# Two tables of step numbers moved, one step reordered and one VectorE job cut in three, in an attention and fp8 layer kernel

## The chip, the core and the metric

The kernel runs on one NeuronCore of a Trainium2 chip. The metric is the device time of one execution in microseconds (us), taken as the median of several runs. Engines are named as the profile names them: PE is TensorE (matrix products and transposes), DVE is VectorE, ACT is ScalarE, POOL is GpSimd, SP is SyncE, which here only issues DMAs. A program on one core has its own instruction order on each engine, and the engines meet through semaphores only.

## What is computed

The input is 8 sequences of 1024 tokens with 256 features. Two residual branches follow each other: attention with distances in hyperbolic space, and one fp8-quantised dense layer. Cut to what matters:

```python
def attn(x):                                   # x: (8, 1024, 256), already layer-normalised; 16 heads of 16
    q_h, k_h, v_h = (exp_map_at_origin(split_heads(x @ W.T), c) for W in (W_q, W_k, W_v))
    dist = poincare_distance(q_h, k_h, c)      # arccosh of 1 + 2c|q-k|^2 / ((1-c|q|^2)(1-c|k|^2))
    weights = softmax(-beta_pos * dist - attention_bias)
    out = log_map(exp_map(weights @ log_map(v_h)))
    return concat(out) @ W_o.T

def ffn(x):                                    # x: bfloat16, layer-normalised
    x_q = (x / s_in).astype(float8_e4m3fn)
    k_q = (kernel / s_k).astype(float8_e4m3fn)
    return ((x_q @ k_q) * (s_in * s_k)).astype(bfloat16) + bias

x = x + attn(layernorm(x))
x = x + ffn(layernorm(x))
```

## The kernel before

**Tiling.** The 8192 tokens are cut into 16 groups of 512 (`NG`, `GTOK`). For each group of query tokens there are 32 steps (`STEPS`): 4 groups of heads times 8 tiles of 128 keys (`KT`). So there are 512 steps, numbered n, and n is also written as group G and step s within the group.

**One step.** PE makes the distances of 128 keys to 512 queries for 4 heads: `distances(n, 0)` and `distances(n, 1)`, two products each (line L1100). ACT takes a logarithm of the 128x2048 tile (`log`, L1217) and then an exponential (`power`, L1224). PE then multiplies the weights with the values (`values`, L1115). ACT thus runs two long instructions for each step. Only where the data could bring an argument near zero are the products bounded first by DVE (`bound`, L1293, and `clamp`, L1302, "open" units of 4 steps); all other units are "closed", and DVE has no work of its own in the attention there. PSUM bank 6 collects the values. The distances use banks 0 to 5, and `distances(n + 1, 1)` and `distances(n + 2, 0)` may be written only when `log(n)` has read its banks (semaphore `freed`).

**The side work.** Beside this, PE has to turn and project the tokens of later groups and to finish earlier groups. All of it goes through the one PSUM bank 7, one use after another: PE fills it, DVE empties it (semaphores `b7_filled` and `b7_copied`), and a later fill waits until the copy before it has ended. The kinds of uses are: X (4 PE transposes of the normalised tokens, two uses a group), M (a projection of 128 tokens onto 384 columns, two products, eight uses a group), A and R (maxima, and transposes of query and key rows), S (the transpose of a finished group of heads' sums, always in steps 2, 10, 18 and 26), T, W, Q and Y (the finishing stage of an earlier group). In which slot each use stands is written by hand in tables: `PROJECT_USES` for groups 3 to 15, `SECOND_USES` for group 2, `FIRST_USES` for what is left of group 1, `FINISH_USES` for the last stage. Group n is projected while group n - 2 is in its steps, and for groups 3 on slot k is step k - 4, so that slot 4 is step 0. For group 2, worked on during group 0, slot and step have the same number. A use written as `(slot, BOTH)` is cut in two: half its products stand ahead of `values` and half behind. `(slot, 0)` puts it whole ahead of `values`, `(slot, 1)` whole behind. In a step without uses PE makes two products whose result nobody reads (`keep_busy`, L1138), except where the step is in `BARE`.

**DVE's order.** In its step n DVE does `rest(n - 1)`: first the copies out of bank 7 of step n - 1's uses, then the copy of the sums (`copy_sums`, L1308, every eighth step), then pieces of the finishing stage (`finish.vector`) and of the projection (`project.vector`), by their own slot numbers. The piece of the finishing stage in slot 33 (step 1) adds bias and residual (L782 and L785); slots 0 to 2 of the projection normalise the tokens (L570 to L581, `xn_rdy`), and X waits for slot 2. After step 12 of group 0 `setup.vector_kernel` quantises the dense layer's weights, seven DVE instructions one behind the other (L236, L109 to L112, L238, L239); its result is first needed when group 0 is finished, long after.

**Group 0.** At step 2 of group 0 PE does what is left of group 1: A 0, R 4 and A 1, all ahead of `values`, and `distances(4, 0)` comes behind R 4, since it reads the keys that R 4 turns. The two DVE pieces that normalise group 2's tokens (slots 0 and 1) come after the copies of that step, and slots 2 and 3 after step 3's.

## Time and profile before

| | us |
|---|---|
| median of 3 runs | 1964.94 |
| lowest and highest of them | 1962.69 and 1970.7 |
| the profiled execution, its own time | 1962.98 |
| its span in the trace | 1961.1 |
| ACT busy | 1865.9 (95%) |
| PE busy | 1750.4 (89%), granted clock 0.981 in the mean |
| DVE busy | 1144.5 (58%) |

The span is the time from the first to the last instruction, and 1.9 us lie around it. Busy time of PE is modelled, so its share says little of what PE could still take. An idle time in brackets stands in front of an instruction, and the arrow names what ended it. The granted clock is TensorE's: 1.00 is 2.4 GHz, 0.50 is 1.2 GHz, and a value between says that part of the stretch had the one and part the other.

### The profile page before, as it was taken

The page shows a single profiled execution, that of the slowest core. Times are in us where ns is not written, and L with a number is a line of the kernel's source. Part 1 is how long each engine was busy: PE and PEld are TensorE (multiplying, and loading weights), DVE is VectorE, ACT ScalarE, POOL GpSimd, SP SyncE. Part 2 cuts the span into 40 slices and gives each one's busy share as a digit, 9 for nine tenths or more (in the row PEclk, how much of TensorE's full clock was granted, in tenths as well). Part 3 has the DMA queues.
Part 4 walks back from the last instruction along what each step waited for, and adds up shares of the span by engine and source line. Part 5 has one row for each costly group of instructions (what it writes and reads, how often), then busy time and mean ns, then how long its engine had stood idle before and what let it go on. Part 6 is the DMA issues. An engine that isn't in the chain of part 4 may idle for free.

```text
span 1961.1 us, 29119 instructions
## 1 busy us (share of the span) xinstructions
PE 1750.4 (89%) x10579; PEld 578.4 (29%) x10579; DVE 1144.5 (58%) x2855; ACT 1865.9 (95%) x1094; POOL 12.9 (1%) x35
## 2 busy tenths in 40 slices
PE   7988989899898898989898898998989899899896
PEld 4323222222222222222222222222222222223234
DVE  7554565665656756565666656656565655513545
ACT  4889999999999799999998899999999999999993
POOL 2000000000000000000000000000000000000000
PEclk9899999999999899999999899999999999999998
DMA  1323222041302214022130321314022131401110
GB/s 57 114 75 115 61 87 93 23 135 44 127 31 87 71 44 136 23 101 79 43 115 22 103 76 44 114 44 136 23 103 77 44 103 44 125 27 39 44 55 23
DMA packets 112953, 142.52 MB, mean 73 GB/s; under 512 B 35692, under 2 KB 61549, under 8 KB 112749
## 3 DMA queue, kind: packets, MB, share of 16 engines
q1 hardware_dynamic: 112748, 140.13, 21.9%
q8 instruction: 88, 1.44, 0.3%
q14 instruction: 117, 0.95, 0.2%
HBM read 85.07 MB, written 55.05 MB: 71 GB/s over the span
## 4 chain that ended last, share of the span: by engine, by line
ACT 55%; PE 21%; issue 14%; DVE 6%; ACTq 2%; DMA 0%; DVEq 0%; SPq 0%
ACT U L1217 29%; ACT U L1224 26%; PE ps L1100 8%; PE ps L402 7%; PE ps L1115 5%; ACTq L1265 2%; DVE U L1302 1%; DVE U L1293 1%; PE ps L407 1%; ACT e L530 0%; DMA U<-in_L_attn_W_o_dram 0%; ACTq L1266 0%; DVE ss L536 0%; PE ps L171 0%; ACTq L1216 0%
## 5 line engine op out<-in xcount | busy, mean ns | idle before, releaser
L1224 ACT ACTIVATE U<-U 128x2048 f32<-128x2048 f32 x512 | 1017.4, 1990 | 0.3
L1217 ACT ACTIVATE U<-ps 128x2048 f32<-128x2048 f32 x500 | 975.7, 1951 | 20.1 <-PE ps L1100 17.6
L1100 PE MATMUL ps<-q_T,k_T 18*128 18x512 f32 x4096 | 634.3, 646 | 142.4 <-ACT U L1217 118.4
L1115 PE MATMUL ps<-U,vals 128*32 128x512 f32 x4096 | 553.7, 613 | 29.3 <-ACT U L1224 28.6
L1100 PEld LDWEIGHTS ps<-q_T,k_T 18*128 18x128 f32 x4096 | 201.5, 186 | 370.3 <-ACT U L1217 324.9
L402 PE MATMUL ps<-wT,xnT 128*128 128x384 f32 x512 | 228.7, 538 | 1.9 <-ACT xnT L463 1.6
L491 DVE COPY qkv<-ps 128x384 f32<-128x384 f32 x112 | 62.4, 557 | 233.6 <-PE ps L402 233.6
L1115 PEld LDWEIGHTS ps<-U,vals 128*32 128x32 f32 x4096 | 81.5, 109 | 204.3 <-ACT U L1224 176.4
L402 PEld LDWEIGHTS ps<-wT,xnT 128*128 128x128 f32 x512 | 79.7, 191 | 193.1 <-issue 120.1
L407 PE MATMUL ps<-ident,rows 128*128 128x128 f32 x512 | 107.4, 309 | 5.4 <-DVE qkv L491 2.4
L407 PEld LDWEIGHTS ps<-ident,rows 128*128 128x128 f32 x512 | 55.1, 147 | 178.7 <-issue 117.2
L499 DVE COPY q_T<-ps 128x512 f32<-128x512 f32 x60 | 41.4, 689 | 82.4 <-PE ps L407 81.8
L726 DVE TENSOR_TENSOR fi_x<-fi_xt,ps 128x256 f32<-128x256 f32 x60 | 25.3, 421 | 103.7 <-PE ps L698 103.7
L698 PE MATMUL ps<-woT,fi_ocT 128*128 128x256 f32 x240 | 83.9, 431 | 0.0
L1308 DVE COPY OTs<-ps 128x512 f32<-128x512 f32 x64 | 43.7, 683 | 54.5 <-PE ps L1115 43.1
L1138 PE MATMUL ps<-woT,ident 128*128 128x256 f32 x216 | 75.3, 431 | 0.0
L501 DVE COPY k_T<-ps 128x512 f32<-128x512 f32 x60 | 41.5, 692 | 48.3 <-PE ps L407 47.8
L698 PEld LDWEIGHTS ps<-woT,fi_ocT 128*128 128x128 f32 x240 | 35.7, 188 | 95.8 <-issue 62.4
L1316 DVE TENSOR_REDUCE den<-ps 128x16 f32<-128x256 f32 x64 | 27.1, 423 | 52.3 <-PE ps L1124 44.6
L1138 PEld LDWEIGHTS ps<-woT,ident 128*128 128x128 f32 x216 | 32.3, 188 | 85.5 <-issue 72.5
L589 DVE TENSOR_REDUCE ss<-sqr 128x48 f32<-128x768 f32 x56 | 53.4, 953 | 1.9
L588 DVE TENSOR_TENSOR sqr<-qkv 128x768 f32<-128x768 f32 x56 | 53.1, 949 | 0.0
(210 smaller groups left out, 1176.5 us busy)
## 6 DMA issues: line engine op xcount, KB each, us to landing
rqb<-q_scratch SPq DMA_DIRECT2D x64, 1024.0 KB, 5.6
q_scratch<-q_T SPq DMA_DIRECT2D x16, 1024.0 KB, 4.5
k_scratch<-k_T SPq DMA_DIRECT2D x16, 1024.0 KB, 7.1
v_scratch<-vals SPq DMA_DIRECT2D x16, 768.0 KB, 4.1
fi_xt<-in_L_attn_x_dram SPq DMA_DIRECT2D x17, 512.0 KB, 5.4
xt<-in_L_attn_x_dram SPq DMA_DIRECT2D x15, 512.0 KB, 6.2
out_dram<-fi_x SPq DMA_DIRECT2D x15, 512.0 KB, 3.7
rk_scratch<-rk SPq DMA_DIRECT2D x16, 32.0 KB, 8.3
```

The source lines that it names most:

```text
L402: ins = pe.matmul(bank[:, 0:384], xnT[:, dc, t * P:(t + 1) * P], g.wT[:, dc, half * 384:(half + 1) * 384], start=dc == 0, stop=dc == 1)
L407: ins = pe.transpose(bank[:, t * P:(t + 1) * P], rows[:, qk, t, hg * HPG:(hg + 1) * HPG, :].rearrange("p h r -> p (h r)"), g.ident[:, :])
L491: v.tensor_copy(qkv[:, t, 24 * half:24 * (half + 1), :].rearrange("p h d -> p (h d)"), bank[:, 0:384]).then_inc(a.b7_copied, 1)
L588: step(v.tensor_tensor(sqr[:, :], src, src, ALU.mult))
L589: step(v.tensor_reduce(ss[:, t, :], sqr[:, :].rearrange("p (h d) -> p h d", d=DH), AX.X, ALU.add))
L698: ins = pe.matmul(bank[:, 0:D], ocT[:, dc, i * P:(i + 1) * P], g.woT[:, dc, :], start=dc == 0, stop=dc == 1)
L1100: ins = pe.matmul(g.ps[:, 2 * pair + i, :], a.k_T[HB * h:HB * h + RD, b % 2, hg, kt * P:(kt + 1) * P], a.q_T[HB * h:HB * h + RD, G % 3, hg ...
L1115: ins = pe.matmul(g.ps[HB * h:HB * h + VW, 6, :], a.vals[:, b % 2, kt, (hg * HPG + h) // 2, DH * (h % 2):DH * (h % 2) + VW], U[:, n % RING ...
L1138: pe.matmul(g.ps[:, 7, 0:D], g.ident[:, :], g.woT[:, 0, :], start=True, stop=True)
L1217: act.activation(U[:, n % RING].rearrange("p b n -> p (b n)"), chunk(n), ACT.Ln, scale=-2.0 / EPS, bias=1.0).then_inc(freed, 1)
L1224: act.activation(U[:, n % RING], U[:, n % RING], ACT.Exp, scale=exponent).then_inc(exp_done, 1)
L1308: v.tensor_copy(OTs[:, :], g.ps[:, 6, :]).then_inc(ot_done, 1)
```

## The change

It does three things.

1. It moves uses of bank 7 to other slots. X 0 and X 1 stand both in slot 4, X 0 whole ahead of `values` and X 1 whole behind; M 0 moves from slot 7 to 5, M 1 from 8 to 7, M 2 from 9 to 8, M 3 from 11 to 10, M 4 from 12 to 11; M 5, M 6 and M 7 stay. In group 2's table M 3, M 4 and M 5 have slots 9, 11 and 12. Bare steps, in which no product fills the gap, are 5 and 8 and no longer 6.
2. At step 2 of group 0, A 0 goes ahead of `distances(3, 1)`, A 1 goes behind `values(1)`, and `distances(4, 0)` goes behind A 1, to the end of the step.
3. `vector_kernel` is cut in three parts, which run after steps 6 (three instructions), 14 (two) and 20 (two) of group 0.

```diff
--- before.py
+++ after.py
@@ -49,9 +49,9 @@
 EARLY = 4
 PROJECT_SLOTS = 37
 FINISH_SLOTS = 35
-PROJECT_USES = {("X", 0): (4, BOTH), ("X", 1): (5, BOTH),
-                ("M", 0): (7, BOTH), ("M", 1): (8, BOTH), ("M", 2): (9, BOTH), ("M", 3): (11, BOTH),
-                ("M", 4): (12, BOTH), ("M", 5): (13, BOTH), ("M", 6): (15, BOTH), ("M", 7): (16, BOTH),
+PROJECT_USES = {("X", 0): (4, 0), ("X", 1): (4, 1),
+                ("M", 0): (5, BOTH), ("M", 1): (7, BOTH), ("M", 2): (8, BOTH), ("M", 3): (10, BOTH),
+                ("M", 4): (11, BOTH), ("M", 5): (13, BOTH), ("M", 6): (15, BOTH), ("M", 7): (16, BOTH),
                 ("R", 0): (25, BOTH), ("R", 1): (26, 0), ("A", 0): (26, 1), ("R", 2): (27, BOTH),
                 ("R", 3): (28, BOTH), ("R", 4): (29, BOTH), ("R", 5): (31, BOTH),
                 ("R", 6): (32, 0), ("A", 1): (32, 1), ("R", 7): (33, BOTH)}
@@ -59,19 +59,19 @@
 FINISH_USES = {("T", 0): (13, BOTH), ("T", 1): (14, BOTH), ("W", 0): (15, BOTH), ("W", 1): (16, BOTH),
                ("W", 2): (17, BOTH), ("W", 3): (19, BOTH),
                ("Q", 0): (30, BOTH), ("Y", 0): (31, 0), ("Y", 1): (31, 1)}
-BARE = (6,)
+BARE = (5, 8)
 
 SHORT_SLOTS = {20: (20, 21, 22), 21: (23, 24), 22: (25,), 23: (26, 27), 24: (28, 29), 25: (30,), 26: (), 27: (31, 32), 28: (33,),
                29: (34,), 30: (), 31: ()}
 SUM_STEPS = 10
 
 
-FIRST_USES = {("A", 0): (2, 0), ("R", 4): (2, 0), ("A", 1): (2, 0), ("R", 5): (3, BOTH), ("R", 6): (6, BOTH),
+FIRST_USES = {("A", 0): (2, 0), ("R", 4): (2, 0), ("A", 1): (2, 1), ("R", 5): (3, BOTH), ("R", 6): (6, BOTH),
               ("R", 7): (14, BOTH), ("R", 0): (17, BOTH), ("R", 1): (19, BOTH), ("R", 2): (20, BOTH),
               ("R", 3): (21, BOTH)}
 
 SECOND_USES = dict(PROJECT_USES)
-SECOND_USES.update({("M", 2): (9, BOTH), ("M", 3): (11, BOTH),
+SECOND_USES.update({("M", 3): (9, BOTH), ("M", 4): (11, BOTH), ("M", 5): (12, BOTH),
                     ("R", 0): (25, BOTH), ("R", 1): (27, 0), ("R", 2): (27, 1), ("R", 3): (28, 0), ("R", 4): (28, 1),
                     ("R", 5): (29, 0), ("A", 0): (29, 1), ("R", 6): (30, 0), ("A", 1): (30, 1), ("R", 7): (31, BOTH)})
 
@@ -103,13 +103,6 @@
 
     def settle(self):
         self.eng.wait_ge(self.sem, self.start + self.n)
-
-
-def quantise_e4m3fn(v, steps, values, spare, spare2, out):
-    steps(v.tensor_scalar(spare.bitcast(I32), values.bitcast(I32), 0x7F800000, None, ALU.bitwise_and))
-    steps(v.tensor_scalar(spare, spare, 2.0 ** -6, 1.5 * 2.0 ** 20, ALU.max, ALU.mult))
-    steps(v.tensor_tensor(spare2, values, spare, ALU.add))
-    steps(v.tensor_tensor(out, spare2, spare, ALU.subtract))
 
 
 def hold(eng, passed):
@@ -230,13 +223,19 @@
         v.sem_inc(const_rdy, 1)
         own["v"] = step.n
 
-    def vector_kernel(v):
-        step = Steps(v, v_steps, own["v"])
-        v.wait_ge(k_in, 16)
-        step(v.tensor_scalar(kval, kraw.rearrange("p c d -> p (c d)"), g.INV_SK, None, ALU.mult))
-        quantise_e4m3fn(v, step, kval, ktmp, ktmp2, kval)
-        step(v.tensor_scalar(ktmp, kval, 3.4028234e38 / 460.0, 0.0, ALU.mult, ALU.mult))
-        step(v.tensor_tensor(g.kq[:, :, :].rearrange("p c d -> p (c d)"), kval, ktmp, ALU.add))
+    def vector_kernel(v, part):
+        step = Steps(v, v_steps, own["v"] + (0, 3, 5)[part])
+        if part == 0:
+            v.wait_ge(k_in, 16)
+            step(v.tensor_scalar(kval, kraw.rearrange("p c d -> p (c d)"), g.INV_SK, None, ALU.mult))
+            step(v.tensor_scalar(ktmp.bitcast(I32), kval.bitcast(I32), 0x7F800000, None, ALU.bitwise_and))
+            step(v.tensor_scalar(ktmp, ktmp, 2.0 ** -6, 1.5 * 2.0 ** 20, ALU.max, ALU.mult))
+        elif part == 1:
+            step(v.tensor_tensor(ktmp2, kval, ktmp, ALU.add))
+            step(v.tensor_tensor(kval, ktmp2, ktmp, ALU.subtract))
+        else:
+            step(v.tensor_scalar(ktmp, kval, 3.4028234e38 / 460.0, 0.0, ALU.mult, ALU.mult))
+            step(v.tensor_tensor(g.kq[:, :, :].rearrange("p c d -> p (c d)"), kval, ktmp, ALU.add))
 
     def await_constants(eng):
         eng.wait_ge(const_rdy, 1)
@@ -999,7 +998,7 @@
         flat = finish.sq[:, :, :, :].rearrange("p t h d -> p (t h d)")
         setup = setup_stage(nc, ctx, g, U[:, 0:2].rearrange("p r h q -> p (r h q)"), finish.xb[:, 0:2, :],
                             flat[:, 0:2 * D], flat[:, 2 * D:], finish.ocT[:, 0, :])
-        QUERY_STEP, KERNEL_STEP = 3, 12
+        QUERY_STEP, KERNEL_STEPS = 3, (6, 14, 20)
 
         def split(n):
 
@@ -1156,6 +1155,9 @@
                         project.await_largest(pe)
                 for n in range(N):
                     G, s = n // STEPS, n % STEPS
+                    early = in_step(0, 2, 0)[:1] if n == 2 else []
+                    for key in early:
+                        use(*key)
                     if n + 1 < N:
                         distances(n + 1, 1)
                     if n != 2:
@@ -1164,10 +1166,8 @@
                     both += [(kind, m, i) for m, k in finished(G, s) for kind, i in begun(FINISH_USES, k)]
                     if G == 0:
                         both += [(kind, 1, i) for kind, i in begun(FIRST_USES, s)]
-                    for key in in_step(G, s, 0):
+                    for key in in_step(G, s, 0)[len(early):]:
                         use(*key)
-                    if n == 2:
-                        distances(n + 2, 0)
                     for key in both:
                         use(*key, 0)
                     unused = n > 2 and s not in BARE and not in_step(G, s, 0) + in_step(G, s, 1)
@@ -1180,6 +1180,8 @@
                         values(n - 1)
                     for key in in_step(G, s, 1):
                         use(*key, 1 if key in both else None)
+                    if n == 2:
+                        distances(n + 2, 0)
                     if unused:
                         keep_busy(first_use[n])
                 values(N - 1)
@@ -1350,8 +1352,8 @@
                         finish.last_early(v, s)
                     if n == QUERY_STEP:
                         project.scale_rows(v, 1, (0,))
-                    if n == KERNEL_STEP:
-                        setup.vector_kernel(v)
+                    if n in KERNEL_STEPS:
+                        setup.vector_kernel(v, KERNEL_STEPS.index(n))
 
                 def unit(n0, products):
```

What it makes of the order. First PE in group 0, from `values(0)` to the distances of step 3. L412 and L415 are A 0 and A 1, L407 is R 4. Before:

```order
L1115 MATMUL ps<-U,vals 32x512 x4
L1100 MATMUL ps<-q_T,k_T 128x512 x2
L412 MATMUL ps<-ident,amax 32x128
L407 MATMUL ps<-ident,rows 128x128 x4
L415 MATMUL ps<-ident,amax_r 1x32
L1100 MATMUL ps<-q_T,k_T 128x512 x2
L1115 MATMUL ps<-U,vals 32x512 x4
L1100 MATMUL ps<-q_T,k_T 128x512 x4
```

Now:

```order
L1114 MATMUL ps<-U,vals 32x512 x4
L411 MATMUL ps<-ident,amax 32x128
L1099 MATMUL ps<-q_T,k_T 128x512 x2
L406 MATMUL ps<-ident,rows 128x128 x4
L1114 MATMUL ps<-U,vals 32x512 x4
L414 MATMUL ps<-ident,amax_r 1x32
L1099 MATMUL ps<-q_T,k_T 128x512 x6
```

The distances of two products that stood alone ahead of `values(1)` are now the first two of six behind it.

Second, PE at the start of a group from group 2 on, steps 0 to 3 (L398 is X, L1124 is S, L402 is M). Before:

```order
L398 MATMUL ps<-ident,xt 128x128 x2
L1115 MATMUL ps<-U,vals 32x512 x4
L398 MATMUL ps<-ident,xt 128x128 x2
L1100 MATMUL ps<-q_T,k_T 128x512 x4
L398 MATMUL ps<-ident,xt 128x128 x2
L1115 MATMUL ps<-U,vals 32x512 x4
L398 MATMUL ps<-ident,xt 128x128 x2
L1100 MATMUL ps<-q_T,k_T 128x512 x4
L1124 MATMUL ps<-ident,OTs 128x128 x4
L1115 MATMUL ps<-U,vals 32x512 x4
L1100 MATMUL ps<-q_T,k_T 128x512 x4
L402 MATMUL ps<-wT,xnT 128x384
```

Now:

```order
L397 MATMUL ps<-ident,xt 128x128 x4
L1114 MATMUL ps<-U,vals 32x512 x4
L397 MATMUL ps<-ident,xt 128x128 x4
L1099 MATMUL ps<-q_T,k_T 128x512 x4
L401 MATMUL ps<-wT,xnT 128x384
L1114 MATMUL ps<-U,vals 32x512 x4
L401 MATMUL ps<-wT,xnT 128x384
L1099 MATMUL ps<-q_T,k_T 128x512 x4
L1123 MATMUL ps<-ident,OTs 128x128 x4
L1114 MATMUL ps<-U,vals 32x512 x4
L1099 MATMUL ps<-q_T,k_T 128x512 x4
L401 MATMUL ps<-wT,xnT 128x384
```

Step 0 holds both X, step 1 the first M. Behind S, the M of steps 3 and 4 stand alone; step 5 is bare, 6 and 7 are M, 8 is bare, 9 is M, 10 is S, and 11 and 12 are M. Before, steps 3, 4 and 5 were M, 6 was bare, 7, 8 and 9 were M, 10 was S, and 11 and 12 were M.

Third, DVE in group 0 from the copies of M 4 on, where the unit is closed. Before:

```order
L491 COPY qkv<-ps 128x384 x2
L588 TENSOR_TENSOR sqr<-qkv 128x768
L589 TENSOR_REDUCE ss<-sqr 128x48
L236 TENSOR_SCALAR fi_osq<-fi_xb,sc 128x512
L109 TENSOR_SCALAR fi_osq<-fi_osq 128x512
L110 TENSOR_SCALAR fi_osq<-fi_osq 128x512
L111 TENSOR_TENSOR fi_ocT<-fi_osq 128x512
L112 TENSOR_TENSOR fi_osq<-fi_ocT,fi_osq 128x512
L238 TENSOR_SCALAR fi_osq<-fi_osq 128x512
L239 TENSOR_TENSOR kq<-fi_osq 128x512
L491 COPY qkv<-ps 128x384
```

Now the first part, behind R 6's copy at step 6:

```order
L500 COPY k_T<-ps 128x512
L230 TENSOR_SCALAR fi_osq<-fi_xb,sc 128x512
L231 TENSOR_SCALAR fi_osq<-fi_osq 128x512
L232 TENSOR_SCALAR fi_osq<-fi_osq 128x512
L1385 UNCONDITIONAL_BRANCH
```

The copy of the M of step 13 stood behind all seven; now two or three of them stand behind a copy of rows, and the step after it has its product at its end. The other engines' orders are the same in both kernels, but for line numbers.

## Rows read from the trace of the kernel before

**Rows 1.** The page, part 1: busy time of each engine.

```profile
PE 1750.4 (89%) x10579; PEld 578.4 (29%) x10579; DVE 1144.5 (58%) x2855; ACT 1865.9 (95%) x1094; POOL 12.9 (1%) x35
```

**Rows 2.** Stretches: length, busy PE, PEld, DVE, ACT, POOL, PEclk, DMA share, GB/s.

```profile
64.50:68.00 3.50, 3.50 (x16) 0.52 (x8) 2.81 (x17) 0.00 (x0) 0.00 (x0) 0.50 0.02 5
...
113.50:117.00 3.50, 3.50 (x11) 1.00 (x10) 0.69 (x1) 1.40 (x1) 0.00 (x0) 0.50 0.04 9
...
155.00:170.00 15.00, 13.62 (x99) 5.06 (x91) 8.83 (x22) 15.00 (x10) 0.00 (x0) 1.00 0.34 107
354.00:472.00 118.00, 106.91 (x666) 33.96 (x666) 70.04 (x175) 117.84 (x69) 0.00 (x0) 1.00 0.23 75
```

**Rows 3.** Timeline of ACT, group 4, logarithms of steps 4, 5, 6, 10, 11.

```profile
533.83 2.04 ACT L1217 ACTIVATE U<-ps 128x2048 f32<-128x2048 f32 x1
...
537.39 2.05 ACT L1217 ACTIVATE U<-ps 128x2048 f32<-128x2048 f32 x1
...
541.14 1.88 ACT L1217 ACTIVATE U<-ps 128x2048 f32<-128x2048 f32 x1
...
555.60 1.88 ACT L1217 ACTIVATE U<-ps 128x2048 f32<-128x2048 f32 x1
...
559.35 1.88 ACT L1217 ACTIVATE U<-ps 128x2048 f32<-128x2048 f32 x1
```

**Rows 4.** Timeline of PE, group 4: distances of steps 1, 3, 4, 5, a half M.

```profile
525.23 1.24 PE L1100 MATMUL ps<-q_T,k_T 18*128 18x512 f32 x8 [0.33 <-ACT U L1217]
...
532.36 1.24 PE L1100 MATMUL ps<-q_T,k_T 18*128 18x512 f32 x8 [0.70 <-ACT U L1217]
533.53 0.91 PE L402 MATMUL ps<-wT,xnT 128*128 128x384 f32 x2
...
536.21 1.14 PE L1100 MATMUL ps<-q_T,k_T 18*128 18x512 f32 x8
...
539.96 1.14 PE L1100 MATMUL ps<-q_T,k_T 18*128 18x512 f32 x8
```

**Rows 5.** Timeline of DVE, group 4: values' scaling, X 1's copy, last of S.

```profile
522.78 1.29 DVE L606 TENSOR_TENSOR vals<-qkv,vg 128x512 f32<-128x512 f32 x2
...
528.50 0.69 DVE L488 COPY xnT<-ps 128x512 f32<-128x512 f32 x1 [2.28 <-PE ps L398]
...
532.48 0.49 DVE L1320 TENSOR_TENSOR on<-ps,den 128x128 f32<-128x128 f32 x2
```

**Rows 6.** Timeline of all engines, group 0, steps 12 to 18.

```profile
106.88 0.48 DVE L236 TENSOR_SCALAR fi_osq<-fi_xb,sc 128x512 f32<-128x512 bf16 x1
...
109.25 1.88 ACT L1217 ACTIVATE U<-ps 128x2048 f32<-128x2048 f32 x1
...
111.57 0.44 PE L407 MATMUL ps<-ident,rows 128*128 128x128 f32 x2 [2.36 <-DVE qkv L491]
...
125.16 1.88 ACT L1217 ACTIVATE U<-ps 128x2048 f32<-128x2048 f32 x1
```

**Rows 7.** Timeline of all engines, group 0, steps 2 to 6.

```profile
60.43 1.88 ACT L1217 ACTIVATE U<-ps 128x2048 f32<-128x2048 f32 x1
...
62.11 2.08 PE L1100 MATMUL ps<-q_T,k_T 18*128 18x512 f32 x4
...
68.11 1.88 ACT L1217 ACTIVATE U<-ps 128x2048 f32<-128x2048 f32 x1 [4.00 <-PE ps L1100]
...
71.22 0.69 DVE L501 COPY k_T<-ps 128x512 f32<-128x512 f32 x1 [3.49 <-PE ps L407]
71.83 1.37 DVE L581 TENSOR_SCALAR xt<-xt,mv,rstd 128x256 f32<-128x256 f32 x4
...
76.34 1.87 ACT L1217 ACTIVATE U<-ps 128x2048 f32<-128x2048 f32 x1
```

**Rows 8.** Timeline of PE, group 0, step 28: a use of four transposes.

```profile
164.21 0.66 PE L407 MATMUL ps<-ident,rows 128*128 128x128 f32 x4
```

**Rows 9.** Timeline of ACT, group 5, behind the open unit of steps 4 to 7.

```profile
677.92 1.88 ACT L1217 ACTIVATE U<-ps 128x2048 f32<-128x2048 f32 x1 [2.09 <-PE ps L1100]
```

## The prediction

> **What bounds the kernel now.** I read the busy times first, then the stretches, then ACT's timeline for places where it departs from its rhythm. ACT is busy for 95% of the span [rows 1], and in a plain stretch for 117.84 of 118 us [rows 2]. So only what makes ACT wait counts, and PE and DVE matter where they are late for it. An undisturbed step takes 537.39 - 533.83 = 3.56 us of ACT. The trace departs from that in four kinds of places: runs of M in each group, steps 12 to 17 of group 0, steps 3 to 5 of group 0, and the open units. The change touches all four, the last only by its side.
>
> **What a run of M costs.** Distances may start when the logarithm before them has ended, and the next logarithm needs them. In step 3 PE waited 0.70 us for ACT and began at 532.36; the next distances began 3.85 us later, at 536.21, and the next at 539.96, 3.75 us later, with no wait at all [rows 4]. So an M step is 3.75 us of PE, 3.85 behind a wait, against 3.56 of ACT. PE falls back by 0.29 in the first M and by 0.19 in each further one. ACT's next logarithm comes 3.75 behind the last, at 541.14, so it has lost 0.19, and its duration falls from 2.05 to 1.88 [rows 3]. That drop matters. In ACT's timeline the durations creep up from 1.88 by some 0.01 a step as long as nothing stops ACT, so instructions end at intervals of about 3.565 while they start at 3.557. A delay of a start that only takes 2.05 back to 1.88 therefore costs nothing at the ends, and distances wait for ends. Of the 0.19 + 0.19 behind steps 4 and 5, 0.17 was such slack and about 0.2 was a loss. The second run, steps 7 to 9, loses 559.35 - 555.60 = 3.75, again 0.19, and only behind its third M. How much lateness is free, then: the distances begun at 536.21, 0.29 late, were just ready for ACT at 537.39, so about 0.27 costs no start, and the duration takes another 0.17: some 0.42 together. Two M make 0.48 and cost about 0.05, three make 0.67 and cost 0.2 to 0.25. Two runs of three cost 0.4 us a group.
>
> **Part 1, the slots, groups 1 to 13.** Runs of three M become runs of one and two. If nothing else happened, this would give 0.4 us in each of 13 groups, 5.2 us. But the new order makes two waits for DVE.
> - Step 0. X 1 cannot be turned before X 0 is copied out of bank 7. At this point DVE is busy with the scaling of values, which began at 522.78 and takes 1.29 us [rows 5], to 524.07. The copy takes 0.69, so X 1 starts at 524.9, takes 0.6 to 0.66 [rows 8], and PE is free at 525.5, where its distances now begin at 525.23 [rows 4]: 0.27 late. M 0 follows in step 1 with 3.75, which makes 0.27 + 0.19 = 0.46. That is at the edge of 0.42, about 0.04 lost. S in step 2 needs far less PE time than 3.56 (PE waited 0.70 behind it), so the lateness is gone by step 3.
> - Steps 1 to 3. M 0's fill ends at about 529.25, where X 1's ended at 528.4. Behind its copy come DVE's bias and residual, then the sums of S, and only then may bank 7 be filled by M 1. In the trace that chain runs from 528.50 to 532.48 + 0.49 = 532.97, 4.47 us [rows 5]; M 1 was filled from 533.53 [rows 4], so 0.56 were to spare. Now it starts at 529.35 and is 0.13 shorter (an M's copy for an X's), so it ends at 533.7, and 0.1 later PE may go on: 0.25 late. With the two M of steps 3 and 4: 0.25 + 0.29 + 0.19 = 0.73, less 0.42 free, is 0.3 lost.
> The other runs (6 and 7, 11 and 12) cost 0.05 each or nothing. Working through all steps in this way I come to 0.2 us gained a group. Ends: 0.4 if neither wait appears, and -0.2 if the chain ends 0.4 us later than I think. Thirteen groups: **2.6 us**, between -2.6 and 5.2. Group 0 has three M in steps 7 to 9 as before and loses the M in step 13; I take 0.
>
> **Part 2, the weights.** The seven DVE instructions begin at 106.88; PE's turn of R 7 then waits 2.36 us for the copy behind them [rows 6]. PE idled, and in the stretch behind it the granted clock was 0.50, which is 1.2 GHz [rows 2]. From 109.25 to 125.16, three steps, ACT needs 15.91 us instead of 3 x 3.557 = 10.67: **5.2 us** lost. In three pieces the longest stands 1.5 us on DVE, behind a copy whose successor is filled at the end of a step, 3 us or more later. I find nobody waiting for it at steps 6, 14 and 20, and the load of the weights has landed long before. This cover holds unless DVE is over 1.5 us behind there. What remains of the 5.2: 0 to 0.5.
>
> **Part 3, step 2.** From the logarithm at 60.43 to that at 76.34, again three steps, 15.91 us are used: 5.2 lost, 4.00 of it as one wait [rows 7]. `distances(4, 0)` stood alone at 62.11, behind A 1's wait for R 4's copy, and took 2.08 us at the low clock; `values(1)` and the next distances came behind. In the new order `values(1)` fills the wait, and the distances of step 4 can follow the end of the logarithm, 60.43 + 1.88 = 62.31, with 1.2 us at the full clock: 63.5, ahead of 63.98, when ACT can take it. So the 4.00 goes. **But then the normalised tokens are late.** DVE was through with the pieces of slots 0 and 1 at 71.22 - 3.49 = 67.73, and then waited for PE [rows 7]. That part of its chain starts from A 1, and moves up by 0.4 at most, to 67.3. Behind it stand R 5's copy, 0.69, and the 1.37 of the normalisation: X 0 may start at 69.4. PE would be there at 67.1. It waits 2.3 us; then X 0, `values`, X 0's copy (behind another DVE instruction like that of [rows 5]), X 1 and distances end at about 73.0. The logarithm of step 6 comes at 73.0 instead of 76.34, a gain of 3.3 at the full clock.
> That wait is as long as the 2.36 of [rows 6], behind which the clock fell. If it falls here too, the X pair, M 0 and two sets of distances run at half speed. PE is then the bound, and a stretch like that behind 113.50 cost ACT 5.2 less the wait itself, some 3 us. So the gain is **0.3**, between -1.5 (a longer low stretch, as at 64.50, [rows 2]) and 3.3. I take the fall, since the nearest row has it.
>
> **The open unit of group 5.** Steps 4 to 7 are open there, and DVE, not PE, sets their time. The new slots take one copy of 0.5 us out of that chain. Behind it PE works at the low clock and ACT waits 2.09 us [rows 9]; step 8, now bare, needs less PE. I take 0.8, between 0 and 2.7.
>
> **The sum.** 2.6 + 5.2 + 0.3 + 0.8 = 8.9 us, off the profiled execution's 1962.98: 1954.1. The median of the runs lies 2 us above that execution, and their spread of 8 us is of the size of one or two low stretches more or less, so I add nothing and say **1954**.
>
> **Rivals.**
> - *The clock stays up at step 4.* For it: PE is busier just before than it was, since the gaps around A 0 and A 1 are filled. Against it: the wait of 2.3 us. Part 3 then gives 3.3: 1962.98 - 11.9 = 1951. Chance 0.25.
> - *The two waits for DVE eat the slots' gain.* If the chain behind M 0 ends 0.2 us later than worked out, part 1 is 0: 1962.98 - 6.3 = 1956.7. For it: DVE's instructions follow closely there, and the margin was only 0.56. Chance 0.2.
> - *The change undoes its own gain in group 0*: the waits at step 4 and the low clock last over 10 us, or DVE is behind at step 6. Parts 2 and 3 together give 2, part 1 2.6 or less: 1957 to 1960. Chance 0.1.
> - *Slower: turning eight times in one step lets the clock fall in each group.* X 0 and X 1 make a step whose PE work is transposes, but for the distances and values. If transposes did not hold the clock, it would fall behind step 0, and M 0 and the M of steps 3 and 4 would run at half speed: about 3 us in each of 13 groups, 39 us, against 8.9: 1993. It decides from the third group in which it happens. Against it: steps 27 to 29 of group 0 hold eight transposes each, and the clock was 1.00 from 155 to 170 [rows 2]. Chance 0.03. The Trainium skill, TensorE: Matmul & The Clock Gate, Part 4, says that transposes do not count as busy for the clock as other products do; by that rule this rival would be likely, but the stretch named speaks against it.
> - *That the change doesn't do what it says* is excluded for the order, which the listing shows; the rest, 0.02.
> Forecast: 0.4.
>
> **How the numbers follow.** The likeliest case is 1954, its own range 1952 to 1956. 1951 and 1956.7 are taken in, and so is the third rival; with the ends of part 1 and of the open unit this gives 1947 to 1960. A measurement of this kernel can tell about 0.5%, 9.8 us, from no change, so the border lies at 1955.1. Faster: most of the forecast (0.27 of 0.4), the first rival (0.25) and a little of the second (0.03) make 0.55. Slower by over 0.5%: 0.04. Within: 0.41.
>
> **What would show it.** Part 1: in groups 2 to 13 the distance from one logarithm to the next is 3.75 once or not at all per group instead of three times, a group takes 0.2 us less than its 32 steps did, and M 1's first product waits for DVE's L1320 (now two lines on). Part 2: no wait of over 1 us for DVE between 80 and 125, and clock 1.00. Part 3: the logarithm of step 4 follows that of step 3 by under 4 us, X 0 waits some 2.3 us for the normalisation, and the clock falls behind it. It would be wrong if X 0 did not wait, if a group took as long as before, or if new low stretches appeared.

## The result and the profile after

The kernel after takes 1956.94 us (median; 1951.58 to 1962.26), the kernel before beside it 1965.26 (1962.69 to 1970.88). The ratio is 0.9949, with a 95% interval of 0.9937 to 0.9961. The interval lies wholly below 1, so the kernel after is faster, by some 10 us. The forecast, 1954, is 3 us too low, and the stated range of 1947 to 1960 holds the result. The profiled execution took 1957.33 us, its span 1955.4.

A ratio here isn't the quotient of the two medians, and for small gains the two differ: 10 us by the ratio are 8.3 in the medians here, and for the weights alone, below, 4.5 and 2.6. "By the ratio" means 1 less the ratio, times the median of the kernel before beside it. Of the twelve executions of the kernel with the order of step 2 alone, one took 8517 us, in a slower state, and the ratio leaves it out.

The page, part 1, of the kernel after (answers to [rows 1]), and the stretch of plain groups that [rows 2] end with:

```profile
PE 1743.8 (89%) x10575; PEld 576.6 (29%) x10575; DVE 1143.3 (58%) x2855; ACT 1864.1 (95%) x1094; POOL 12.9 (1%) x35
```

```profile
354.00:472.00 118.00, 107.09 (x670) 34.04 (x666) 70.25 (x177) 117.99 (x68) 0.00 (x0) 1.00 0.24 77
```

ACT is still the bound, and its idle time in that stretch has gone from 0.16 us to 0.01. From the timelines of ACT I took the distance from the first logarithm of each group to that of the next:

| part of the program | before, us | after, us | gained |
|---|---|---|---|
| start to the first logarithm | 45.49 | 45.11 | 0.4 |
| group 0, steps 0 to 2 | 14.94 | 14.60 | 0.3 |
| group 0, steps 3 to 8 | 26.58 | 25.85 | 0.7 |
| group 0, steps 9 to 14 | 22.24 | 22.05 | 0.2 |
| group 0, steps 15 to 17 | 15.91 | 10.70 | 5.2 |
| group 0, steps 18 to 31 | 50.11 | 50.11 | 0.0 |
| eleven plain groups of 1 to 13, but 8 | 1262.54 | 1259.47 | 3.1 |
| group 5 | 126.08 | 123.25 | 2.8 |
| group 8 | 128.51 | 128.03 | 0.5 |
| group 14 | 113.81 | 113.81 | 0.0 |
| group 15, 31 steps | 113.31 | 120.62 | -7.3 |
| the end | 41.58 | 41.81 | -0.2 |

So 13.2 us were gained up to the end of group 14, more than the 8.9 of the forecast, and 7.3 were lost in group 15, of which the forecast has nothing. The first row says little: in the traces of all kernels below, the first logarithm comes at 45.1 to 47.8 us.

**Plain groups.** ACT, group 4 (start, duration), against [rows 3]; then PE and DVE, against [rows 4, 5]:

```profile
526.05 2.04 ACT L1219 ACTIVATE U<-ps 128x2048 f32<-128x2048 f32 x1
...
529.72 1.94 ACT L1219 ACTIVATE U<-ps 128x2048 f32<-128x2048 f32 x1
...
533.47 1.88 ACT L1219 ACTIVATE U<-ps 128x2048 f32<-128x2048 f32 x1
```

```profile
516.96 0.66 PE L397 MATMUL ps<-ident,xt 128*128 128x128 f32 x4 [0.21 <-DVE xnT L487]
...
524.58 1.24 PE L1099 MATMUL ps<-q_T,k_T 18*128 18x512 f32 x8 [0.55 <-ACT U L1219]
525.86 0.91 PE L401 MATMUL ps<-wT,xnT 128*128 128x384 f32 x2
```

```profile
525.26 0.49 DVE L1322 TENSOR_TENSOR on<-ps,den 128x128 f32<-128x128 f32 x2
```

The distances from one logarithm to the next are 3.67 and 3.75 us behind steps 4 and 5, and at most 3.60 elsewhere in the first half of the group; before there were three of 3.75. X 1 waits 0.21 for X 0's copy. The chain behind M 0 ends at 525.26 + 0.49 = 525.75, and M 1 starts 0.11 later. That is 1.28 us after the start of the distances ahead of it, where the M in the same place started 1.17 after them [rows 4], so M 1 is some 0.1 late.

**Group 0, steps 4 to 6,** PE and ACT:

```profile
69.84 0.79 PE L397 MATMUL ps<-ident,xt 128*128 128x128 f32 x4 [3.06 <-DVE xt L580]
```

```profile
67.19 1.87 ACT L1219 ACTIVATE U<-ps 128x2048 f32<-128x2048 f32 x1
...
74.68 1.88 ACT L1219 ACTIVATE U<-ps 128x2048 f32<-128x2048 f32 x1 [3.83 <-PE ps L1099]
```

```profile
71.00:74.50 3.50, 3.50 (x20) 1.06 (x12) 1.12 (x2) 0.00 (x0) 0.00 (x0) 0.63 0.41 105
```

The wait of 4.00 [rows 7] is gone, and a wait of 3.06 for the normalisation stands in its place, with a low clock behind it (0.63 in the mean of the stretch).

**Group 5,** ACT at the end of the open unit, and the last stretch but one of the unit, against [rows 9]:

```profile
662.07 1.91 ACT L1214 ACTIVATE U<-U 128x2048 f32<-128x2048 f32 x1 [2.04 <-DVE U L1304]
663.88 1.86 ACT L1219 ACTIVATE U<-ps 128x2048 f32<-128x2048 f32 x1
```

```profile
657.00:660.50 3.50, 3.50 (x15) 0.71 (x10) 3.40 (x7) 3.00 (x2) 0.00 (x0) 0.54 0.00 0
```

The columns of the stretch are those of [rows 2]. The low clock comes inside the unit here, where ACT waits for DVE anyway, and behind the unit ACT no longer waits for PE.

**Group 15.** Stretches of the kernel after, steps 5 to 11 (columns as in [rows 2]):

```profile
1814.00:1817.50 3.50, 2.24 (x20) 0.57 (x16) 0.59 (x1) 3.50 (x3) 0.00 (x0) 1.00 0.00 0
...
1824.50:1828.00 3.50, 2.24 (x22) 0.57 (x16) 0.69 (x1) 3.50 (x3) 0.00 (x0) 1.00 0.01 2
1828.00:1831.50 3.50, 3.50 (x18) 0.70 (x10) 0.00 (x0) 3.50 (x3) 0.00 (x0) 0.50 0.02 5
1831.50:1835.00 3.50, 3.50 (x14) 1.02 (x10) 0.00 (x0) 1.20 (x1) 0.00 (x0) 0.50 0.00 0
```

Here no M stands in any step, and steps 5 and 8, bare now, leave PE 2.24 us of work in 3.5. Behind the second of them the clock goes to 0.50 (1.2 GHz), and in the second stretch at that clock ACT is busy for 1.20 of 3.5. This is only half of what the group lost. Steps 12 to 15 are an open unit here, and up to its first logarithm 3.55 us were lost. The other 3.76 were lost from there on, at a second low clock, for instance in this stretch:

```profile
1858.50:1862.00 3.50, 3.50 (x18) 1.02 (x10) 0.85 (x2) 1.64 (x1) 0.00 (x0) 0.50 0.00 0
```

Just ahead of that one stands no bare step, but two waits of PE for DVE, of 0.93 us and this:

```profile
1854.68 1.69 PE L1099 MATMUL ps<-q_T,k_T 18*128 18x512 f32 x8 [1.53 <-DVE U L1304]
```

Whether the low clock would have come there without the bare steps isn't shown.

### The profile page after: what moved, and what is told of

The parts are those of the page before. It is cut to its first block, busy times and chain, and to the rows that moved or that the text cites. A ratio compares the mean times of both kernels' runs of the same rounds, so it can differ in the third digit from the quotient of the medians.

```text
span 1955.4 us, 29112 instructions
## 1 busy us (share of the span) xinstructions
PE 1743.8 (89%) x10575; PEld 576.6 (29%) x10575; DVE 1143.3 (58%) x2855; ACT 1864.1 (95%) x1094; POOL 12.9 (1%) x35
## 4 chain that ended last, share of the span: by engine, by line
ACT 64%; issue 21%; DVE 7%; PE 5%; ACTq 3%; DMA 0%; DVEq 0%; SPq 0%
ACT U L1226 34%; ACT U L1219 29%; ACTq L1267 2%; PE ps L1099 2%; PE ps L1114 1%; DVE U L1304 1%; DVE U L1295 1%; PE ps L401 1%; DVE ss L535 0%; ACT e L529 0%; PE ps L697 0%; ACTq L1268 0%; DMA U<-in_L_attn_W_o_dram 0%; PE ps L406 0%; DVE vals L605 0%
```

## The experiments

Two questions: do the three parts give what the sum says, each by itself and together, and are the bare steps what group 15 paid for? All ratios are against the kernel before, run beside each experiment in five rounds. In the traces I give the time of group 0's steps 3 to 8 (26.58 us before, 25.85 after), that of its steps 15 to 17 (15.91, 10.70), and what groups 14 and 15 lost together against the 227.12 that they took before.

### Each part alone

The slots alone: the three tables of slots of the change and no other line. The core of it:

```diff
-PROJECT_USES = {("X", 0): (4, BOTH), ("X", 1): (5, BOTH),
+PROJECT_USES = {("X", 0): (4, 0), ("X", 1): (4, 1),
-BARE = (6,)
+BARE = (5, 8)
-SECOND_USES.update({("M", 2): (9, BOTH), ("M", 3): (11, BOTH),
+SECOND_USES.update({("M", 3): (9, BOTH), ("M", 4): (11, BOTH), ("M", 5): (12, BOTH),
```

> The kernel before with the three tables of slots of the change alone (the turns of the tokens, and with them the bare steps 5 and 8 in place of 6). Theory A, that the parts add and that the bare steps are what group 15 pays for: groups 1 to 13 give the 6.4 us that they give in the trace of after (0.27 a group, 2.8 in group 5), and group 15 takes back up to 7.3 us, because steps 5 and 8 do without the turns that keep PE busy where no M stands in them. In the profile, start of group 15 some 6 us earlier than before, and its 32 steps 120 to 121 us long where they were 113.3. Time: within 2 us of before, ratio 0.999 to 1.001. Rival B, that group 15 of after was slow by chance and not by its bare steps: ratio 0.9965 to 0.997, group 15 at 113.3 us. Rival C, that the slots gain only together with part 3 (both change how late PE enters group 1): groups 2 to 13 at 114.79 us as before.

Measured: 1954.88 us, ratio 0.9938 (0.9919 to 0.9957), which is no theory's figure: the slots alone give as much as the whole change. In the trace groups 1 to 13 gave 6.8 us, about the 6.4 that A and B had, groups 14 and 15 lost 1.0, and steps 15 to 17 of group 0 took 10.71 us though the weights' seven instructions still stand in one piece. (The profiled execution itself is only 4.6 us shorter than that of before: steps 3 to 8 took 4.8 us more in it and the start 2.0 more, which later traces show to vary by themselves.) DVE's timeline of this kernel, and PE's:

```profile
117.13 0.69 DVE L239 TENSOR_TENSOR kq<-fi_osq 128x512 bf16<-128x512 f32 x1
118.33 0.69 DVE L501 COPY k_T<-ps 128x512 f32<-128x512 f32 x1 [0.51 <-DVE kq L239]
```

```profile
110.38 0.91 PE L402 MATMUL ps<-wT,xnT 128*128 128x384 f32 x2
...
115.62 0.44 PE L407 MATMUL ps<-ident,rows 128*128 128x128 f32 x2
```

And DVE's timeline of the kernel before, at the same place (what [rows 6] leave out):

```profile
110.23 0.69 DVE L239 TENSOR_TENSOR kq<-fi_osq 128x512 bf16<-128x512 f32 x1
110.96 0.56 DVE L491 COPY qkv<-ps 128x384 f32<-128x384 f32 x1
```

Before, the copy of the M in step 13 stood behind the seven instructions, and R 7 in step 14 needs the bank that it empties. The new table has no M in step 13. So there is no copy to wait for: the last M's copy ran at 111.33, ahead of the seven (they begin at 113.77 in this trace), and R 7 starts at 115.62 without a wait. The 5.2 us belong to part 1 as much as to part 2.

The weights alone: steps 6, 14 and 20 in place of 12.

```diff
-        QUERY_STEP, KERNEL_STEP = 3, 12
+        QUERY_STEP, KERNEL_STEPS = 3, (6, 14, 20)
```

> The kernel before with the weights' quantisation in three pieces at steps 6, 14 and 20 alone. The sum says 5.2 us, less 0 to 0.5: ratio 0.9972 to 0.9978, steps 15 to 17 of group 0 at 3.56 us each instead of 6.35, 5.81 and 3.75, no wait of PE for DVE of over 1 us between 80 and 125, and the clock at 1.00 there. The steps 2 to 5 of group 0 stay as they were. Rival: the piece at step 6 comes where DVE is late in this kernel, since here the turns of step 2 are still stacked; then PE waits over 1 us at step 6 or 7 and at most 3 us are gained, ratio 0.9985 or more.

Measured: 1962.18 us, ratio 0.9977 (0.9963 to 0.9990), 4.5 us. Steps 15 to 17 took 10.70 us, as worked out, and PE waited for DVE for 0.37 us at most between 80 and 125 us. The rival falls. Steps 3 to 8 took 30.90 us in this trace against 26.58, with the old order in both; more of that below.

The order of step 2 alone:

```diff
+                    early = in_step(0, 2, 0)[:1] if n == 2 else []
+                    for key in early:
+                        use(*key)
...
-                    if n == 2:
-                        distances(n + 2, 0)
```

> The kernel before with the new order of step 2 alone (the first turn and values in front of the distances, which come last). Theory A: the wait of 4.00 us at step 4 goes, and about 3 us of it come back at step 6, where X and M work behind a wait for the normalisation at the low clock; X 0 stands in step 4 here and X 1 in step 5, so that the low stretch falls on both. Gain 0.3 to 1.7 us, ratio 0.9991 to 0.9999; steps 15 to 17 of group 0 stay slow (6.35, 5.81, 3.75). Rival: with X 0 and X 1 in different steps the clock doesn't fall, and the gain is 3.3, ratio 0.9983.

Measured: 1963.01 us, ratio 0.9984 (0.9971 to 0.9997), 3.1 us. Steps 3 to 8 took 26.68 (3.66, 3.57, 7.87, 4.45, 3.57, 3.56): the wait at step 4 is gone and 5.2 us come back at steps 5 and 6. The trace agrees with A, the ratio with the rival. The interval takes in both, so this run tells only that something is gained.

### Two parts together

The slots and step 2, with the weights in one piece at step 12 (the diff of the weights above, undone in the kernel after):

> The kernel after with the weights' quantisation in one piece at step 12, as before: the slots and the order of step 2 alone. Theory A, from the trace of the slots alone: there the seven instructions stand in one piece too, and steps 15 to 17 of group 0 took 3.56, 3.55 and 3.60 us all the same, since no M stands in step 13 any more and R 7 comes a step's worth of PE's own time later; so the pieces add nothing to the slots. Time as that of after, ratio 0.994 to 0.9955, steps 15 to 17 at 3.55 to 3.60 us. Rival, the prediction's sum: the pieces are worth 5.2 us on top, ratio 0.9975, steps 15 to 17 at some 6.3, 5.8 and 3.75.

Measured: 1954.28 us, ratio 0.9935 (0.9920 to 0.9951), steps 15 to 17 at 3.55, 3.56 and 3.60. The pieces add nothing to the slots, and the prediction's sum, which has them as its largest term, falls as an account of this change.

The weights and step 2, with the slots as before:

> The kernel before with the weights in pieces and the order of step 2, without the slots. If these two parts add (4.5 and 3.1 us by themselves): 7.6 us, ratio 0.996. If each of them only shortened the same low stretches in group 0, 4 to 5 us: 0.9975. Groups 1 to 13 as before, 114.79 us each, group 5 about 126, group 15 at 113.3.

Measured: 1958.85 us, ratio 0.9960 (0.9945 to 0.9975). These two add (4.5 + 3.1 = 7.6; measured 7.9). Group 15 took 113.30.

### The last groups

The kernel after, with the turns that keep PE busy in the last two groups' steps 5 and 8 too:

```diff
-                    unused = n > 2 and s not in BARE and not in_step(G, s, 0) + in_step(G, s, 1)
+                    unused = n > 2 and (s not in BARE or G >= LAST - 1) and not in_step(G, s, 0) + in_step(G, s, 1)
```

> The kernel after, with turns that keep PE busy also in steps 5 and 8 of the last two groups, where no M stands. Theory A (the bare steps let the clock fall there): group 15 takes 113.3 to 114 us instead of 120.6, the low stretch of 10.2 us that begins at 1828 in the profile of after is gone, and the low stretch behind the open unit, from 1855, is as it may be. Time 1950 to 1953, ratio against before 0.9925 to 0.9935. Rival B (the low stretches fell there by chance, and come and go from run to run): the time is as that of after, ratio 0.9949, and a low stretch of 10 us is still found between steps 5 and 10 of group 15 in about as many runs.

Measured: 1955.30 us, ratio 0.9942 (0.9923 to 0.9961). The low stretch at steps 8 to 10 isn't there and the last groups lost 0.86 in place of 7.3, as A says. But the time is that of after, as B says.

The kernel before, with 5 and 8 bare there in place of 6:

> The kernel before with steps 5 and 8 of the last two groups bare, in place of step 6; nothing else is changed, and no turn of tokens moves. Theory A (two bare steps three apart let the clock fall): group 15 is 3 to 7 us longer than 113.3, and the ratio is 1.0015 to 1.0035. Rival B (chance): ratio 0.9995 to 1.0005.

Measured: 1967.47 us, ratio 1.0008 (0.9998 to 1.0019). The profiled execution lost 4.8 us in the last groups, behind step 5 of group 14 this time:

```profile
1719.50:1723.00 3.50, 2.24 (x18) 0.50 (x18) 1.23 (x1) 3.50 (x3) 0.00 (x0) 1.00 0.01 5
1723.00:1726.50 3.50, 3.50 (x14) 1.08 (x18) 0.00 (x0) 3.50 (x3) 0.00 (x0) 0.58 0.00 0
```

What the last groups lost in the profiled executions of all kernels: with steps 5 and 8 bare 7.3, 7.4, 4.8, 2.6, 1.0, 1.0 and 1.0 us; with 6 bare or none 0, 0, 0, 0, 0.86, 0.86 and 0.86. Not all of this can be put down to the bare steps. Up to the first logarithm of group 15's open unit the seven with 5 and 8 bare lost 3.6, 3.6, 4.0, 2.6, 1.0, 1.0 and 1.0, and none of the seven others lost more than 0.03. That difference is what the bare steps cost in these executions. From the open unit on it is 3.8, 3.8, 0.8, 0, 0, 0 and 0 in the seven, and 0 four times and 0.8 or 0.9 three times in the others. A loss there comes without bare steps 5 and 8 too, so nothing here shows that the 3.8 of after is theirs. By the ratios the cost of the bare steps isn't clear of nothing: 1.4 us between after and the kernel with turns in these steps, and 1.6 for the kernel before with 5 and 8 bare, where the interval goes up to 3.7. So a loss of 7 us can't be the rule.

### Two attempts at more

The finishing piece that stands ahead of S's normalisation, one slot later:

```diff
-        if k == 33:
+        if k == 34:
```

> The kernel after with one piece of DVE's finishing work (the bias and the residual, slot 33) a slot later, behind the normalisation by S and not ahead of it, so that bank 7 is free for M 1 about 0.5 us sooner. By the prediction's sum, where M 1's wait of 0.25 us costs a group 0.2: 1.3 to 2.6 us less than after. By what the trace of after shows (M 1 waited about 0.1 us, and a group gained 0.27 already): at most 0.05 a group, 0.7 us in all, which can't be told from none. The log distances of steps 4 and 5 of a group tell: 3.67 and 3.75 in after; if the first is 3.56 and the second 3.75 or less, the wait is gone.

Measured: 1953.42 us, ratio 0.9943 (0.9930 to 0.9957), the same as after. Step 4 took 3.56 us in place of 3.67, and the eleven plain groups 1258.4 in place of 1259.5: M 1's lateness was worth 0.1 a group. Group 5 took 1.5 us more. Of that 1.0 is ACT's wait for DVE ahead of the open unit, 3.00 against 2.03, where the piece now stands in DVE's way.

Group 0's X 0 and X 1 a step or two later, behind the normalisation, and R 6 in the gap:

```diff
-("R", 5): (3, BOTH), ("R", 6): (6, BOTH),
+("R", 5): (3, BOTH), ("R", 6): (4, 1),
-SECOND_USES.update({("M", 3): (9, BOTH), ("M", 4): (11, BOTH), ("M", 5): (12, BOTH),
+SECOND_USES.update({("X", 0): (5, 1), ("X", 1): (6, 0), ("M", 0): (7, BOTH), ("M", 1): (8, BOTH), ("M", 2): (9, BOTH),
+                    ("M", 3): (11, BOTH), ("M", 4): (12, BOTH), ("M", 5): (13, BOTH),
```

> The kernel after with the turns of group 0 changed alone: X 0 of the second group stands in step 5 and X 1 in step 6 instead of both in step 4, M 0 to M 5 in 7, 8, 9, 11, 12 and 13, and R 6 in step 4. Theory A (step 6's 7.49 us are X 0's wait for the normalisation and the low clock behind it): X 0 no longer waits, steps 5 and 6 take 3.6 to 3.9 us each, and 3 to 4 us are gained, ratio against after 0.998, and 0.993 against before. Rival: DVE's chain from A 1 to the normalisation is what is late wherever X 0 stands, or the two M more in a row give it back in steps 7 to 9; then under 1 us is gained.

Measured: 1948.14 us, ratio 0.9917 (0.9903 to 0.9930), the best of all, and its interval lies apart from that of after. PE of this kernel, and the stretch in which the kernel after had 0.63:

```profile
72.52 0.66 PE L398 MATMUL ps<-ident,xt 128*128 128x128 f32 x4
```

```profile
70.50:74.00 3.50, 2.83 (x25) 0.99 (x20) 2.24 (x3) 3.50 (x3) 0.00 (x0) 1.00 0.49 160
```

X 0 waits for nothing, and steps 3 to 8 take 21.45 us, of which 21.3 are ACT's own (6 x 3.557). That is 4.4 us less than in the trace of after, a little over the 3 to 4 of A; with an M in step 13 again, 0.2 of it came back in steps 9 to 14. Between the two ratios lie 6.3 us.

The three edits together:

> The three edits to the kernel after together: turns that keep PE busy in steps 5 and 8 of the last two groups, the finishing piece a slot later, and group 0's X a step or two later. If each does what its theory says, they add: 3 to 7 us from group 15, 3 to 4 from group 0, 0 to 2 from the finishing piece, so 1944 to 1950, ratio 0.989 to 0.992. If they don't add, because a clock that stays up in one place falls in another: 0.993.

Measured: 1948.20 us, ratio 0.9922 (0.9909 to 0.9936): group 0's gain is there, the other two give nothing that can be measured. With the best kernel's slots and step 6 bare in the last two groups (step 6 in place of steps 5 and 8, `BARE if G < LAST - 1 else (6,)`):

> The kernel with group 0's X 0 and X 1 in steps 5 and 6 (weights in three pieces), and in the last two groups step 6 bare as in the kernel before, in place of 5 and 8. Theory A (two bare steps without an M leave PE too idle; one does not): groups 14 and 15 take 113.81 and 113.31 us, as in the four profiles that have step 6 bare there, where those with 5 and 8 bare lost 1.0 to 7.3 us in one of them. The other kernel's runs at 1948.1 to 1948.5 hold the small loss of 1.0, so 1947 to 1948, ratio 0.991, and no run over 1950. Rival B (the loss comes and goes with the moment at which the clock's low stretches end, whatever step is bare): no difference from 0.9917, and groups 14 and 15 lose 0 to 1 us as before.

Measured: 1951.85 us, ratio 0.9926 (0.9901 to 0.9950). The profiled execution lost 0.86 us in group 15, in a step behind the open unit, where the theory had 0, and its runs reach 1957.87. A falls in the form in which I gave it. Ahead of the open unit nothing was lost, which is the part of it that holds.

Last, the best kernel with the weights in one piece, which puts an M in step 13 behind the seven instructions again:

> The kernel with X 0 and X 1 of group 0 in steps 5 and 6 and M 5 in step 13 again, with the weights' quantisation in one piece at step 12. Theory A (it is M 5's place, and not the rest of the slots, that makes the one piece cheap): PE's turn of R 7 waits about 2.4 us again, steps 15 to 17 of group 0 take some 6.3, 5.8 and 3.75 us, and the time is 5.2 us over that of the same kernel with the weights in pieces: 1953, ratio against before 0.9943. Rival (something else in the slots does it): steps 15 to 17 at 3.56 and ratio 0.9917.

In the profiled execution A's mechanism is there in full, in PE's timeline and in the stretch behind it:

```profile
106.58 0.44 PE L408 MATMUL ps<-ident,rows 128*128 128x128 f32 x2 [2.36 <-DVE qkv L492]
```

```profile
109.50:113.00 3.50, 3.50 (x11) 0.95 (x10) 0.69 (x1) 1.44 (x1) 0.00 (x0) 0.50 0.02 5
```

Steps 15 to 17 took 7.30, 6.43 and 3.74 us, 6.8 more than in the best kernel, so it is M 5's place. But the expected price of 5.2 isn't in the ratio: the time is 1950.07 us, the ratio 0.9916 (0.9900 to 0.9931), where the best kernel has 0.9917. The median itself is 1.9 us above the best kernel's, but the two were taken on different chips, and the kernel before beside it was 2.8 higher too, so a loss of about 2 us can't be ruled out. The profiled execution took 1960.11 at a mean clock of 0.978, the six others 1949.18 to 1951.88 at 0.987, which is the clock of the best kernel. The 10 us between them aren't the price of M 5's place alone, since the profiled execution also lost 7.4 in groups 14 and 15, where the best kernel lost 1.0. The order of instructions is the same in all seven, so the wait for the copy should be there each time, and it seems that the clock fell behind it in one of seven. Of the six others only the mean clock is known, so this is an inference.

## Why the prediction came out

**The sum is near, its account is not.** 8.9 us were forecast against 8.3 in the medians, 10 by the ratio, and 5.7 in the profiled executions. That the number is so near is in part luck: in the traces 13.2 us were gained and 7.3 lost where the forecast had nothing, and the largest term belongs to part 1 as much as to part 2. Step by step:

- *The cost of a run of M* and the slack of 0.42 us: right. A plain group gained 0.27, where 0.2 was worked out; M 1 was late by about 0.1 and not by 0.25, and taking that away gave 0.1 a group. A plain group has one distance of 3.75 where it had three, as forecast.
- *"Group 0 has three M in steps 7 to 9 as before and loses the M in step 13; I take 0"*: this step failed. That M's copy was the one that R 7 waited for. I had read the wait for the copy in [rows 6], and had put the new M table beside it without asking whether that copy is still there. Part 1 by itself was worth 12 us by the ratio (8 to 16; in the trace 5.2 in steps 15 to 17 and 6.8 in groups 1 to 13, less 1.0 at the end), not 2.6 + 0.8, and part 2 on top of it nothing that can be told from none (0.9949 with the pieces, 0.9935 without).
- *Part 2*: its mechanism, its place and its size (5.2, 5.2 measured in the trace) were right for the part alone. Counting it beside part 1 was right too, as long as part 1 was held to give nothing there; the two errors cancel in the sum.
- *Part 3*: 0.3 was taken. X 0 waited 3.06 us, not 2.3, and the clock fell, as forecast. Steps 3 to 8 took 26.58, 30.89, 30.90 and 31.37 us in the four traces with the old order of step 2 (the last with the new slots), and 25.85, 28.22, 28.29 and 28.30 in the four that have the new order with the change's own slots: 2.3 us gained in the mean, inside the range. Alone the part gave 3.1 by the ratio, with an interval from 0.6 to 5.7. What it gives on top of the slots (0.9935 against 0.9938) isn't told apart from nothing.
- *The open unit*: 0.8 was taken, and group 5 gained 2.8 in the trace of after and 0.3 to 2.2 in the eight others with the new slots. In most the term was too small. Step 8, behind the unit, took 3.55 to 3.75 us in all nine, where it was 5.77.
- *The bare steps*: the prediction counted step 8 bare as a gain and didn't ask what the two bare steps do in groups without an M. In groups 14 and 15 no M stands around them, and 1.0 to 4.0 us were lost there ahead of the open unit in the profiled executions with them.
- *The rivals.* The clock did not stay up at step 4. The DVE waits did not eat the slots' gain. The third came true in part: in three of the four traces with the new order and the change's own slots the low clock behind step 4 lasted some 10 us, but DVE was not behind for the weights. Nothing was slower by the transposes. The stretch 354 to 472 holds eight of them in one step of each group at a granted clock of 1.00. By itself that proves little, since the bare steps 5 and 8 stand in the same stretch and didn't bring the clock down there either. The row from 155 to 170 [rows 2] says more, though the prediction read it a little wrong: steps 27 and 28 of group 0 hold eight transposes each, but step 29 holds five (R 5 and A 0). Steps 26 to 29 have nothing but transposes beside the distances and the values, and the clock was 1.00. By the rule of the Trainium skill, TensorE: Matmul & The Clock Gate, Part 4, that transposes don't count as busy for the clock, it should have been low there, at least as much as behind the bare steps of group 15; the trace speaks against the rule in this mix.

## What to carry over

When two edits each remove the same wait, each by itself gets its whole price, and together they get it once (here 5.2 us in the traces of the slots, of the weights, and of both). So name for every stall the one instruction that ends it, and look for it in the order of each part apart, before the gains are added. A filler that keeps an engine busy must be looked at in the first and last groups too, where the work that usually surrounds it is missing: here the clock fell there in each of the seven traces without it in steps 5 and 8, though the times of all runs don't show the cost. And where a new wait takes an old one's place, move the waiting work behind its input: here that gave 4.4 us in the traces, where the change of order itself had given 0.7.

## What was not expected of the hardware

The same wait has not the same price each time. X 0 waits 3.06 us in the kernel after and 3.07 with the slots and step 2. In these stretches of the latter

```profile
72.00:75.00 3.00, 2.37 (x12) 0.92 (x12) 2.31 (x4) 1.64 (x1) 0.00 (x0) 0.50 0.84 258
75.00:78.00 3.00, 3.00 (x16) 1.24 (x12) 0.69 (x1) 0.00 (x0) 0.00 (x0) 0.50 0.33 75
78.00:81.00 3.00, 3.00 (x10) 0.71 (x10) 0.00 (x0) 2.31 (x2) 0.00 (x0) 0.50 1.00 286
```

the clock stays at 0.50 for the 9 us that they span, against the one stretch of 0.63 in the kernel after, and steps 3 to 8 take 28.29 against 25.85. In group 0 of the kernel before, and of a kernel with the same instructions up to group 14, it was 26.58 and 30.89. Of the seven traces with steps 5 and 8 bare, the two that lost over 7 us in group 15 are the two whose first logarithm came at 45.1 us; in the other five it came at 45.6 to 47.8. It looks as if the moment at which a wait falls decides what it costs, but that is a guess from seven traces of different kernels, and the moment wasn't varied by itself. The Trainium skill, TensorE: Matmul & The Clock Gate, Part 1, says that the gate's phase is independent of the kernel's start and that the effect is run-variable; these rows are in line with that, and don't prove it. For an edit of this size it means that one profiled execution gives the mechanism and its place, but not the mean price: 7.3 us in one trace were about 1.5 by the ratios, and 6.8 in another couldn't be found in its ratio and were at most 2 in its median.
